# A graph network with a mixture of experts: the output rows as a product of 16 rows on TensorE

## The reference

```
    v = jnp.clip(ffn_out @ Wv + bv, -V_MAX, V_MAX)
    mask = (scores >= thr[:, None]).astype(x.dtype)
    gr, gi = _bk_gii(v)
    feats = jnp.clip(jnp.stack([gr, gi], -1) * mask[..., None], -FEAT_CLAMP, FEAT_CLAMP)
    return ffn_out + bk_scale * (feats @ Wo + bo)
```

## Time and profile before

| what | value |
|---|---|
| median of the timed runs | 490.38 us (3 runs, 490.18 to 490.52) |
| the profiled execution's own time | 492.77 us |
| its span, from first to last instruction | 490.9 us |
| TensorE busy | 461.6 us, 94% |
| VectorE, ScalarE, GpSimd busy | 128.7, 64.2, 35.0 us |
| moved by DMA | 190.04 MB, 387 GB/s on average |
| mean granted TensorE clock | 0.991 of full speed |

### The profile page before, as it was taken

The page is one execution under the profiler, slowest core; times in us unless marked ns, Lnnn a source line. Parts: engine busy times, 40 slices in busy tenths (PEclk is TensorE's granted clock), DMA queues, the critical chain, the costliest instruction groups (busy, mean ns, idle before and its releaser), DMA issues.

```text
span 490.9 us, 5912 instructions
## 1 busy us (share of the span) xinstructions
PE 461.6 (94%) x2292; PEld 229.5 (47%) x2292; DVE 128.7 (26%) x342; ACT 64.2 (13%) x126; POOL 35.0 (7%) x50
## 2 busy tenths in 40 slices
PE   7999999999999999999999999999999789779881
PEld 5666666667558444344344344344344234224340
DVE  6563677425206320010020010010010011001255
ACT  2011122001003120020020020020020011002200
POOL 3442120000100000000320000000000000000000
PEclk9999999999999999999999999999999999999996
DMA  8989999999999999999999999999999999999800
GB/s 307 402 258 397 404 399 419 414 400 415 422 401 377 359 421 424 422 425 423 404 420 424 423 427 427 422 425 426 424 424 427 425 423 424 428 424 423 345 1 32
DMA packets 32460, 190.04 MB, mean 387 GB/s; under 512 B 5446, under 2 KB 5558, under 8 KB 18108
## 3 DMA queue, kind: packets, MB, share of 16 engines
q1 hardware_dynamic: 31580, 189.74, 94.4%
q0 software_dynamic: 576, 0.06, 0.1%
q10 hardware_dynamic: 288, 0.03, 0.0%
HBM read 189.42 MB, written 0.39 MB: 387 GB/s over the span
## 4 chain that ended last, share of the span: by engine, by line
PE 71%; DMA 15%; SPq 8%; DVE 4%; issue 1%; ACT 0%; DVEq 0%
PE ps L1350 18%; PE ps L1323 17%; PE ps L1099 13%; PE ps L1140 11%; DMA extra<-in_L_ffn_W 7%; DMA lower<-in_L_ffn_W 6%; SPq L333 6%; PE ps L1336 2%; SPq L328 2%; PE ps L1127 2%; PE ps L1278 2%; PE ps L1156 2%; DMA x_sb<-in_x 1%; PE ps L1413 1%; PE ps L1065 1%
## 5 line engine op out<-in xcount | busy, mean ns | idle before, releaser
L1099 PE MATMUL ps<-slot,xT 128*128 128x384 f32 x192 | 65.8, 497 | 0.0
L1323 PE MATMUL ps<-extra,gathered 128*64 128x512 f32 x252 | 56.7, 597 | 4.9 <-DMA extra<-in_L_ffn_W 4.9
L1140 PE MATMUL ps<-slot,eluT 128*128 128x512 f32 (+1 forms) x168 | 55.3, 486 | 0.0
L1323 PE MATMUL ps<-left,gathered 128*64 128x512 f32 x216 | 49.3, 597 | 5.2 <-DMA left<-in_L_ffn_W 4.8
L902 DVE TENSOR_TENSOR hidden<-ps,b_T 128x384 f32<-128x384 f32 x32 | 16.9, 555 | 122.8 <-PE ps L1336 122.8
L1099 PEld LDWEIGHTS ps<-slot,xT 128*128 128x128 f32 x192 | 36.4, 194 | 23.8 <-issue 1.5
L1350 PE MATMUL ps<-lower_2nd,hidden 128*64 128x384 f32 x252 | 43.2, 490 | 2.5 <-DMA lower_2nd<-in_L_ffn_W 2.5
L1140 PEld LDWEIGHTS ps<-slot,eluT 128*128 128x128 f32 x168 | 31.5, 190 | 22.2 <-issue 20.1
L1350 PE MATMUL ps<-lower,hidden 128*64 128x384 f32 x216 | 36.8, 489 | 1.2 <-DMA lower<-in_L_ffn_W 1.0
L1350 PE MATMUL ps<-lower_on,hidden 128*64 128x384 f32 x216 | 37.5, 492 | 0.0
L1323 PEld LDWEIGHTS ps<-extra,gathered 128*64 128x64 f32 x252 | 17.0, 137 | 39.1 <-issue 29.9
(11 more groups left out here) (323 smaller groups left out, 338.7 us busy)
## 6 DMA issues: line engine op xcount, KB each, us to landing
slot<-in_L_gnn_W SPq DMA_DIRECT2D x31, 1152.0 KB, 13.9
extra<-in_L_ffn_W SPq DMA_DIRECT2D x21, 1536.0 KB, 21.1
left<-in_L_ffn_W SPq DMA_DIRECT2D x18, 1536.0 KB, 22.8
lower_2nd<-in_L_ffn_W SPq DMA_DIRECT2D x21, 1152.0 KB, 23.6
lower<-in_L_ffn_W SPq DMA_DIRECT2D x18, 1152.0 KB, 9.7
lower_on<-in_L_ffn_W SPq DMA_DIRECT2D x18, 1152.0 KB, 25.5
chunk<-in_L_ffn_W SPq DMA_DIRECT2D x9, 1536.0 KB, 9.7
lower_extra<-in_L_ffn_W SPq DMA_DIRECT2D x7, 1152.0 KB, 22.6
```

The source lines that it names most:

```text
L1099: last = T.matmul(ps[:, 2 * (h % 2) + b, 0:HB], xT[:, 3 * half + k, :], slots[n % RING][:, k, b * HB:(b + 1) * HB], start=(n % 2 == 0 and ...
L1140: last = T.matmul(ps[:, b, 0:end - first], elu_part(KT * h + 3 * half + k, 1)[:, 0, :], slots[n % RING][:, k, first:end], start=(h == 0 an ...
L1323: last = T.matmul(ps[b * CAP:(b + 1) * CAP, s, 0:BANK], gathered[:, k, :], upper_homes[k][:, at:at + BANK], start=(k == 0), stop=(k == KT ...
```

## The change

The last stage is written as a product. With 16 rows on the contraction side (2 parts x 8 steps), the output rows are features (16 x 128 nodes) times Wo (16 x 768).

- `wo_rows` becomes 16 x 768: row 0 of Wo on partitions 0 to 7 and row 1 on 8 to 15, by two loads that repeat a row. GpSimd no longer spreads or scales it.
- ScalarE makes `own_signed` (128 x 2 x 8): `own_step` times bk_scale and times -bk_scale. TensorE turns it to 16 x 128 into `ps[:, 1]`, behind the bias product, and ScalarE copies it to `own_T`.
- `cf_g` is kept with the parts outside and the steps inside, and is clamped before it goes to the nodes.
- The `to_nodes` product has its operands exchanged, so its result is 16 x 128. VectorE multiplies it by `own_T` (`cf_f`, semaphore `features`).
- TensorE adds `cf_f` times `wo_rows` to the two accumulators. ScalarE copies the left half, VectorE the right, and SP stores each half with a transfer of its own.
- Ahead of L1449 stand 10 fillers instead of 12 (the turn is there too); 7 are added behind L1449 and 2 behind L1454.

```diff
-WARM = (5, 0, 2, 8, 2, 0, 1, 3, 2, 0, 2, 12)
+WARM = (5, 0, 2, 8, 2, 0, 1, 3, 2, 0, 2, 10, 7, 2)
...
# sync
-            sp.wait_ge(final_ready, 1)
-            sp.dma_start(out, xc[:, :]).then_inc(out_done, 16)
-            sp.wait_ge(out_done, 16)
+            for half, ready in ((0, left_ready), (1, right_ready)):
+                sp.wait_ge(ready, 1)
+                sp.dma_start(out[:, half * HB:(half + 1) * HB], xc[:, half * HB:(half + 1) * HB]).then_inc(out_done, 16)
+            sp.wait_ge(out_done, 32)
...
# gpsimd
-                pool.dma_start(wo_rows[0:1, j, :], wo[j:j + 1, :]).then_inc(end_rows_in, 16)
+                pool.dma_start(wo_rows[j * CL:(j + 1) * CL, :], wo[j:j + 1, :].to_broadcast([CL, D])).then_inc(end_rows_in, 16)
...
-            G.partition_broadcast(wo_rows[:, :, :].rearrange("p a c -> p (a c)"),
-                                  wo_rows[0:1, :, :].rearrange("p a c -> p (a c)")).then_inc(end_spread, 1)
             G.partition_broadcast(wv_row[:, :], wv_row[0:1, :]).then_inc(end_spread, 1)
-            pool.wait_ge(end_spread, 1)
-            pool.wait_ge(minus_ready, 1)
-            G.tensor_tensor(wo_rows[:, 1, :], wo_rows[:, 1, :], minus_bk[:, :].to_broadcast([P, D]),
-                            ALU.mult).then_inc(rows_scaled, 1)
...
# scalar
+            act.wait_ge(minus_ready, 1)
+            act.wait_ge(own_kept, 1)
+            S.activation(own_signed[:, 0, :], own_step[:, :], ACT.Identity, scale=bk_c[:, :])
+            S.activation(own_signed[:, 1, :], own_step[:, :], ACT.Identity, scale=minus_bk[:, :]).then_inc(own_scaled, 1)
             act.wait_ge(end_spread, 1)
-            S.activation(wo_rows[:, 0, :], wo_rows[:, 0, :], ACT.Identity, scale=bk_c[:, :]).then_inc(rows_scaled, 1)
-            act.wait_ge(end_spread, 2)
...
             take_y(rounds)
+            act.wait_ge(own_turned, 1)
+            S.copy(own_T[:, :], ps[0:2 * CL, 1, 0:P]).then_inc(own_ready, 1)
+            act.wait_ge(final_sum, 1)
+            S.copy(xc[:, 0:HB], ps[:, 6, 0:HB]).then_inc(left_ready, 1)
...
# vector
-            V.tensor_tensor(cf_g[:, :, :], cf_c[:, :, :], cf_e[:, :].unsqueeze(2).to_broadcast([CH, CL, 2]),
-                            ALU.mult).then_inc(cf_ready, 1)
-
+            step(V.tensor_tensor(cf_g[:, :, :].rearrange("p c j -> p j c"), cf_c[:, :, :],
+                                 cf_e[:, :].unsqueeze(2).to_broadcast([CH, CL, 2]), ALU.mult))
+            V.tensor_scalar(cf_g[:, :, :], cf_g[:, :, :], FCLAMP, -FCLAMP, ALU.min, ALU.max).then_inc(cf_ready, 1)
+
+            dve.wait_ge(own_ready, 1)
             dve.wait_ge(cf_moved, 4)
-            step(V.tensor_tensor(cf_f[:, :, :], ps[:, 5, 0:2 * CL].rearrange("p (j c) -> p j c", j=CL),
-                                 own_step[:, :].unsqueeze(2).to_broadcast([P, CL, 2]), ALU.mult))
-            step(V.reduce_sum(feats[:, :], cf_f[:, :, :].rearrange("p j c -> p c j"), AX))
-            step(V.tensor_scalar(feats[:, :], feats[:, :], FCLAMP, -FCLAMP, ALU.min, ALU.max))
-            dve.wait_ge(rows_scaled, 2)
-            dve.wait_ge(scattered, rounds)
-            dve.wait_ge(bias_added, 1)
-            step(V.scalar_tensor_tensor(out=blocks(xc[:, :]), in0=blocks(wo_rows[:, 0, :]), scalar=feats[:, 0:1],
-                                        in1=ps[:, 6:8, 0:HB], op0=ALU.mult, op1=ALU.add))
-            V.scalar_tensor_tensor(out=xc[:, :], in0=wo_rows[:, 1, :], scalar=feats[:, 1:2], in1=xc[:, :],
-                                   op0=ALU.mult, op1=ALU.add).then_inc(final_ready, 1)
+            V.tensor_tensor(cf_f[:, :], ps[0:2 * CL, 5, 0:P], own_T[:, :], ALU.mult).then_inc(features, 1)
+            dve.wait_ge(final_sum, 2)
+            V.tensor_copy(xc[:, HB:D], ps[:, 7, 0:HB]).then_inc(right_ready, 1)
...
# tensor
+            pe.wait_ge(own_scaled, 1)
+            T.matmul(ps[0:2 * CL, 1, 0:P], own_signed[:, :, :].rearrange("p c j -> p (c j)"), ident[:, :],
+                     start=True, stop=True).then_inc(own_turned, 1)
             stay_warm(WARM[11], 0)
...
+            stay_warm(WARM[12], 0)
             pe.wait_ge(cf_ready, 3)
...
+            stay_warm(WARM[13], 0)
             pe.wait_ge(cf_ready, 4)
-            T.matmul(ps[:, 5, 0:2 * CL], to_nodes[:, :], cf_g[:, :, :].rearrange("p j c -> p (j c)"),
+            T.matmul(ps[0:2 * CL, 5, 0:P], cf_g[:, :, :].rearrange("p c j -> p (c j)"), to_nodes[:, :],
                      start=True, stop=True).then_inc(cf_moved, 1)
+            pe.wait_ge(end_rows_in, 64)
+            pe.wait_ge(features, 1)
+            for b in range(2):
+                T.matmul(ps[:, 6 + b, 0:HB], cf_f[:, :], wo_rows[:, b * HB:(b + 1) * HB], start=False, stop=True,
+                         skip_group_check=True).then_inc(final_sum, 1)
```

More of the change, by code:

```diff
@@ L126, in gnn_moe_kernel @@
         top[0] = moe_base + lower_at[1]
-        wo_rows = place("wo_rows", [P, 2, D])
+        wo_rows = place("wo_rows", [2 * CL, D])
         wv_row = place("wv_row", [P, D])
@@ L135, in gnn_moe_kernel @@
               ("cf_th", [CP, CL + 1, 2]), ("cf_q", [CP, 3, CL, 2]), ("cf_r", [CP, CL]), ("cf_a", [CP, CL, 2]),
-              ("cf_d", [CH, CL, 2]), ("cf_c", [CH, CL, 2]), ("cf_g", [CH, CL, 2]), ("cf_e", [CH, CL]),
-              ("cf_f", [P, CL, 2]), ("cf_pre", [2, GC, GC, 4, 4]), ("cf_px", [2, GC, 4, 2, 4]),
+              ("cf_d", [CH, CL, 2]), ("cf_c", [CH, CL, 2]), ("cf_g", [CH, 2, CL]), ("cf_e", [CH, CL]),
+              ("own_signed", [P, 2, CL]), ("own_T", [2 * CL, P]), ("cf_f", [2 * CL, P]), ("cf_pre", [2, GC, GC, 4, 4]), ("cf_px", [2, GC, 4, 2, 4]),
               ("cf_sx", [2, GC, GC - 1, 4, 4]), ("cf_k", [CP, CL // 2, 16]), ("cf_h", [CP, CL // 2])]
         (cf_w, cf_v, cf_t, cf_m, cf_mm, cf_s, cf_x, cf_n, cf_p, cf_b, cf_y, cf_th, cf_q, cf_r, cf_a,
-         cf_d, cf_c, cf_g, cf_e, cf_f, cf_pre, cf_px, cf_sx, cf_k, cf_h) = [place(*t) for t in tail_tiles]
+         cf_d, cf_c, cf_g, cf_e, own_signed, own_T, cf_f, cf_pre, cf_px, cf_sx, cf_k, cf_h) = [place(*t) for t in tail_tiles]
         assert top[0] <= moe_base + lower_at[1] + 3 * slot
@@ L266, in gnn_moe_kernel @@
         onehot_ready, rank_done, hot_T_ready = sem("onehot_ready"), sem("rank_done"), sem("hot_T_ready")
-        route_ready, score_exp = sem("route_ready"), sem("score_exp")
+        route_ready = sem("route_ready")
         score_ready, score_turned, thr_ready, thr_done = (sem("score_ready"), sem("score_turned"),
@@ L272, in gnn_moe_kernel @@
         turned, biased_ready, gelu_done = sem("turned"), sem("biased_ready"), sem("gelu_done")
-        y_ready, scattered, bias_added = sem("y_ready"), sem("scattered"), sem("bias_added")
+        y_ready, scattered = sem("y_ready"), sem("scattered")
         place_ready, place_turned, place_T_ready = (sem("place_ready"), sem("place_turned"),
@@ L276, in gnn_moe_kernel @@
         gather_done, gathered_ready = sem("gather_done"), sem("gathered_ready")
-        minus_ready, rows_scaled = sem("minus_ready"), sem("rows_scaled")
-        last_dot, last_placed, ffn_scaled, x1_done = sem("last_dot"), sem("last_placed"), sem("ffn_scaled"), sem("x1_done")
+        minus_ready, features = sem("minus_ready"), sem("features")
+        last_dot, last_placed = sem("last_dot"), sem("last_placed")
         first_dot, top_ready, hot_turned = sem("first_dot"), sem("top_ready"), sem("hot_turned")
-        v_ready, v_turned = sem("v_ready"), sem("v_turned")
+        v_ready, v_turned, own_kept = sem("v_ready"), sem("v_turned"), sem("own_kept")
         cf_init, cf_ready, cf_moved = sem("cf_init"), sem("cf_ready"), sem("cf_moved")
-        final_ready, out_done = sem("final_ready"), sem("out_done")
+        final_sum, left_ready, right_ready = sem("final_sum"), sem("left_ready"), sem("right_ready")
+        own_scaled, own_turned, own_ready, out_done = (sem("own_scaled"), sem("own_turned"), sem("own_ready"),
+                                                       sem("out_done"))
         def elu_part(first, n):
@@ L896, in take_threshold @@
                 step(V.tensor_scalar(keep[:, :], col(SCORE), ps[:, 3, HB:HB + 1], None, ALU.is_ge))
-                V.tensor_scalar(own_step[:, :], step_mask[:, :], keep[:, :], None, ALU.mult)
+                V.tensor_scalar(own_step[:, :], step_mask[:, :], keep[:, :], None, ALU.mult).then_inc(own_kept, 1)
             def round_(r, first=False):
@@ L936, in _ @@
             V.tensor_scalar(x1[:, :], x1[:, :], col(MEAN), None, ALU.subtract).then_inc(full_ready, 1)
-            dve.wait_ge(end_spread, 2)
+            dve.wait_ge(end_spread, 1)
             V.tensor_tensor_reduce(out=blocks(junk[:, :]), in0=ps[:, 6:8, 0:HB], in1=blocks(wv_row[:, :]),
@@ L1442, in _ @@
             for b in range(2):
[L1443 to L1446, removed]
+                T.matmul(ps[:, 6 + b, 0:HB], bk_c[0:1, 0:1].to_broadcast([1, P]),
+                         bo_row[0:1, b * HB:(b + 1) * HB], start=False, stop=True,
+                         skip_group_check=True)
```

(3 more changed lines are left out.)

4 lines of the change are left out of this document (2 added, 2 removed).

## The result

| | before | after |
|---|---|---|
| median of the timed runs | 490.45 us (490.18 to 491.74, 4 runs) | 499.23 us (498.89 to 500.84, 4 runs) |
| the profiled execution and its span | 492.77 and 490.9 us | 498.89 and 497.1 us |

The account below looks back on a forecast made before the run. It took the serial chain of waits in the last microseconds, with the store behind it, as the bound. Terms of -0.25 up to the last store's issue and -0.5 for the store gave about -0.8: 489.6 us, range 489.2 to 491.1.

Parts of the forecast that it names:

- item 1: Chain up to L1452 stays: own_signed turn, ScalarE's small steps and GpSimd's removed spread and product all cost 0.
- Items 2: Seven fillers after L1449 and two after L1454 finish before the next products are wanted; cost 0 if the clock holds.
- rival C: Clock falls where it fell before, fillers run slow and delay L1452 by 0.8 us; together +2.3, 491.9 us; chance 0.17.
- one of the prediction's own signs of being wrong: L1452 starting after the end of its VectorE step by more than a handoff.
- C's milder end: The clock falls but the grant comes back during the fillers: about 490.4 to 490.9 us.
- Item 3: Clamp moved ahead of the to_nodes product: one 16x16 VectorE step with its wait, +0.20 us.
- Item 4: to_nodes product with exchanged operands at the full clock: 0.38 us instead of 0.62, -0.24.
- Items 5 to 7: After to_nodes: own_T product 0.31, last product 1.61, second-half copy 0.56; 2.48 against 2.69 us, -0.21.
- Item 8: The last store carries half the bytes, so it ends sooner: -0.5 us taken, bounds 0 and -0.55.
- rival B: The second store, with rows of half the length, isn't shorter: 490.1 us; chance 0.14.
- The new form alone gains nothing: At the tail, a product, a copy and a moved clamp cost what the two VectorE passes did.
- A: The forecast itself, clock held to the end: 489.6 us, in itself 489.2 to 489.9; chance 0.60.

Follow-up runs that it names:

- e2: Before with the scaling of Wo's second row (L478) moved from GpSimd to ScalarE, so GpSimd ends on a spread; ratio to before 1.013.
- f1: After, unchanged, repeated in a second set of runs; ratio to before 1.013.
- e1: After plus a one-column GpSimd product, which nobody reads, behind the last spread (the switch back); ratio to before 0.9997.
- g4: Repeat of e1, unchanged, over 12 runs; ratio to before 0.9997.
- f4: f2 with the output stored by one transfer once both halves are copied; ratio to before 1.0039.
- f2: e1 with 17 fillers instead of 10 in the first gap; ratio to before 1.0038.
- g1: Before with only the store split: second pass in two halves, a transfer behind each; ratio to before 0.9979.
- e3: After with Wv loaded onto all partitions by the transfer and GpSimd's last spread removed; ratio to before 1.0052.
- g2: Before plus a one-column GpSimd spread, which nobody reads, behind its last product; ratio to before 1.0121.

## Why the prediction was wrong

It gave 489.6 us, range 489.2 to 491.1, and 0.14 to slower. It came out 1.7% slower (1.3% in the second comparison), far outside, and no rival held the cause.

**The step that failed is in item 1:** "GpSimd loses the spread L473 and, behind it, the product L478 … two hundred microseconds before their reader: 0". The reader was looked for within the execution. It is the next execution, whose iota runs at once only if the program ends on its kind, as before did with L478. Taking L478 away cost 8.6 to 8.8 us at the start and about 6.4 us of the time (ratio 1.013 in e2, which removes nothing else from GpSimd, and in f1). The trace of before had the warning twice: the idle "issue" of 9.81 us ahead of L478, which the prediction's own view of wo_rows' writers sums to 16.2 us for two, and 9.63 us ahead of the first spread. The Trainium skill (GPSIMD Engine Reference, section "2.1 Instruction dispatch") says that the first call to freshly loaded GpSimd code also pays about 6 us, measured there as 5.95 from MODIFY_POOL_CONFIG to the first instruction, less the wait for events. In this case's rows the same gap is 6.1 us at L473 of before, 8.9 at the start of after, and 9.6 and 9.8 ahead of L438 and L478 of before, so the measurements lie up to 3.9 us above that figure. That the start depends on what the program ended on stands in the runs alone.

**Items 2 and rival C.** The clock was the open question and was put rightly: in after's profile C happened, L1452 late by 0.9 us (C said 0.8), and with it one of the prediction's own signs of being wrong. C's milder end had the grant coming back. It did so at 490.15 us here and at 485.13 in e1, so L1458 took 0.39 and 0.42 us and not 0.62; in g4, the same kernel as e1, it didn't. What no rival had is that it can fall a second time, as at 493.56 us here, and that executions of one kernel differ: one outcome was given to all of them. The tail's +1.1 us, less 0.4 for the store, would by itself have given 491.1 us, the range's upper end.

**Item 3**, the moved clamp: +0.20, measured +0.21.

**Item 4**: the product measures 0.39, as taken (0.38), but the handoff to VectorE adds 0.11, and the term is -0.14 and not -0.24.

**Items 5 to 7**: 2.48 against 2.69 was the forecast. e1's rows give 0.42 (product and handoff, forecast 0.31), 1.52 (1.61), and 0.60 for the copy and its handoff (0.56): 2.54, so -0.15. In after the fall at 493.56 us makes it 2.79.

**Item 8**: the store, -0.5 forecast, -0.4 in rows (f4 against the halves). Those rows refute rival B; the medians of f2 and f4 are too close to tell.

**The sum of the tail**, with the switch put back, was to be -0.8 us. In f2's profile, where everything held, it is 7.16 instead of 7.26 us, and -0.4 for the store: -0.5; over many executions e1 and g4 put the new kernel, store and all, at 0.9997, no gain. The forecast's -0.8 us, a ratio of 0.9984, still lies inside both intervals, so these runs don't exclude it. "The new form alone gains nothing" fits them. The split store is the part that the rows credit, and g1 has it without the product. In the sum the low end is also off: -1.05 from 490.38 is 489.33, and A's range began at 489.2.

What stays open: why executions of before differ by up to 4 us, on what it depends at which gap the grant falls, how the 3.2 us that after recovers divide between the low-level stretch and the transfers, and why some executions of e3, f2 and f4 take longer outside their span.

## What to carry to other kernels

On GpSimd, an instruction's cost includes the idle time behind a change of kind, and the kind of the program's last instruction decides whether the first one of an execution pays it: let a program end on the kind that it begins with, or put a one-column instruction of that kind where GpSimd is idle. When a GpSimd instruction is removed, read the "issue" gap ahead of it and look for MODIFY_POOL_CONFIG rows. Count a filler's delay at the low level too, but don't drop it for that alone: here 7 and 2 late fillers, which held L1452 up by 0.9 us in after's profile, gave 0.9997 with the switch back, 4 and 4 gave 1.0024, and none 1.0034.

## What the runs showed of the hardware

- GpSimd sits idle when it changes between iota or tensor_tensor and a spread, and a program that ends on a spread pays this at the start of its executions, as if the loaded code outlived them. The idle time was 9.3 to 9.9 us at a start, and in the middle between 6.0 us (L474 of g2) and 12.6 us (L478 of g4); on what its length depends was not found.
- A start later by 8.6 to 9.3 us lengthened the time by 5.9 to 6.5 us (some 8 in the first comparison). Of the 8.63 us in after's profile 3.2 came back; weights that have landed meanwhile and a shorter time at the low level fit the rows, but their shares were not measured.
- TensorE's grant in the tail fell at 486.74 us (after), 482.25 (f1, the same kernel), 481.71 (e1), 482.04 (g4, the same kernel as e1) and 473.98 (f4). It came back in all of these but g4 and fell again after 486 us.
- Seven more fillers in the first gap (17 instead of 10) gave 1.0038 and 1.0039 (1.002 by spans alone); without the late ones it was 1.0034; with all as they were 0.9997.
- Half of a store of 384 KB, issued last, is over 2.3 us after its issue, the whole 2.7.
